# Slice weights of a graph network: a third buffer of normalised rows, and another order of the turned tiles on TensorE

## The reference

```python
x_mid = (x @ W_x + b_x).reshape(B, N, H, D).transpose(0, 2, 1, 3)      # H = 8 heads of 64
temp = jnp.clip(temperature, 0.1, 5.0)
slice_weights = jax.nn.softmax((x_mid @ W_slice + b_slice) / temp, axis=-1)
slice_norm = slice_weights.sum(axis=2)
slice_token = jnp.einsum('bhnc,bhng->bhgc', fx_mid, slice_weights)
slice_token = slice_token / (slice_norm[..., None] + 1e-05)
# attention among the 64 slice tokens of each head gives out_slice
out_x = jnp.einsum('bhgc,bhng->bhnc', out_slice, slice_weights)
```

## Time and profile before

| | |
|---|---|
| median of 3 runs | 7850.16 us (7850.01 to 7862.31) |
| the profiled execution, time | 7849.75 us |
| its span in the trace | 7848.0 us |
| busy in the span | PE 69%, DVE 66%, POOL 44%, ACT 24% |
| `slice_weights` | 3558 to 3888 us of the span |

### The profile page before, as it was taken

The page is one execution under the profiler, slowest core; times in us unless marked ns, Lnnn a source line. Parts: engine busy times, 40 slices in busy tenths (PEclk is TensorE's granted clock), DMA queues, the critical chain, the costliest instruction groups (busy, mean ns, idle before and its releaser), DMA issues. The chain is left out here.

```text
span 7848.0 us, 86538 instructions
## 1 busy us (share of the span) xinstructions
PE 5431.4 (69%) x24766; PEld 3747.1 (48%) x24766; DVE 5164.8 (66%) x11681; ACT 1874.3 (24%) x4564; POOL 3485.0 (44%) x3441
## 2 busy tenths in 40 slices
PE   5877774555555555517799788888899999951991
PEld 2446663333333443314464333433777778750661
DVE  6457767888888877774467566676666767660332
ACT  0333332222223333212224200000222222210220
POOL 0000004777777777710000355555666777716006
PEclk8998886777777777759999899999999999965995
DMA  4100003444455555530013322222333333332223
GB/s 143 45 27 1 1 1 95 124 124 124 124 126 128 128 131 129 136 60 3 6 68 132 117 75 73 72 75 77 87 94 94 98 97 97 97 70 83 64 63 107
DMA packets 310188, 665.87 MB, mean 85 GB/s; under 512 B 77974, under 2 KB 173964, under 8 KB 302717
## 3 DMA queue, kind: packets, MB, share of 16 engines
q0 software_dynamic: 180352, 455.22, 23.0%
q1 hardware_dynamic: 129383, 205.31, 7.6%
HBM read 546.52 MB, written 113.55 MB: 84 GB/s over the span
## 5 line engine op out<-in xcount | busy, mean ns | idle before, releaser
L2055 POOL DMA_INDIRECT ag_rows<-table,row_src x1612 | 1595.8, 990 | 1896.5 <-POOLq L2847 1023.5
L1142 POOL DMA_INDIRECT at_rows<-table,row_dst x1612 | 1645.5, 1021 | 491.3 <-issue 450.8
L1308 PE MATMUL at_p_a<-at_rows,at_hot 128*125 128x264 f32 x3224 | 1132.0, 509 | 1014.6 <-issue 972.1
L1308 PEld LDWEIGHTS at_p_a<-at_rows,at_hot 128*125 128x125 f32 x3224 | 706.0, 245 | 1201.7 <-issue 1062.5
L2422 PE MATMUL mo_p_e<-ag_rows,ag_hot 128*125 128x256 f32 x2192 | 650.9, 422 | 293.9 <-DVE acc L2263 257.2
L1271 DVE TENSOR_TENSOR acc<-acc,at_p_a 125x264 f32 x1612 | 687.1, 426 | 245.0 <-PE at_p_a L1308 101.8
L2263 DVE TENSOR_TENSOR acc<-acc,mo_p_e 125x256 f32 x1096 | 459.0, 419 | 442.9 <-PE mo_p_e L2422 243.1
L2422 PEld LDWEIGHTS mo_p_e<-ag_rows,ag_hot 128*125 128x125 f32 x2192 | 391.5, 199 | 503.1 <-DVE acc L2263 394.8
L2165 DVE TENSOR_TENSOR mo_prod<-mo_far,mo_twice 125x256 f32<-125x256 f32 x1600 | 580.4, 419 | 51.6 <-issue 45.1
L1094 POOL PARTITION_ALL_REDUCE sb_top<-sb_top x1 | 0.4, 398 | 1220.8 <-DVE sb_top L1065 1220.8
L1258 DVE TENSOR_TENSOR at_rows<-at_rows 128x1024 f32<-128x1024 f32 x496 | 496.2, 1021 | 21.9 <-ACT at_rows L1190 21.6
(11 more groups left out here) (491 smaller groups left out, 9751.8 us busy)
## 6 DMA issues: line engine op xcount, KB each, us to landing
at_wide<-node_t SPq DMA_DIRECT2D x124, 406.2 KB
table<-rt_row SPq DMA_DIRECT2D x50, 1000.0 KB
at_rows<-table,row_dst POOLq DMA_INDIRECT x1612
ag_rows<-table,row_src POOLq DMA_INDIRECT x1612
moe_in<-ones SPq DMA_DIRECT2D x1, 13440.0 KB
ex_space<-moe_in SPq DMA_DIRECT2D x105, 128.0 KB, 2.2
moe_out<-ex_space SPq DMA_DIRECT2D x105, 128.0 KB, 1.7
table<-row SPq DMA_DIRECT2D x50, 128.9 KB
```

What stands on the lines that cost most here:

```text
L1142: pool.indirect_dma_start(out=rows[n % 3][:, g, :], out_offset=None, in_=m.table0, in_offset=bass.IndirectOffsetOnAxis(ap=row_i[:, n * G + ...
L1308: pe.matmul(p_a[k % BANKS][0:P, 0:TW], hot[n % 2][:, g, :], rows[n % 3][:, g, :], start=True, stop=True).then_inc(s_agg, 1)
L2055: pool.indirect_dma_start(out=rows[:, i % RING, j, :], out_offset=None, in_=m.table1, in_offset=bass.IndirectOffsetOnAxis(ap=row_i[:, 2 * ...
```

## The change

There are three buffers `sl_xn` instead of two. ACT normalises tile n+2 behind exp(n), and copies its turned tile behind swt(n). PE runs logits(n+1), W(n), turn(n+2), S(n) in step n, so that the turned rows are made two tiles ahead and stand between the turned weights and the sums. The two loops of PE, ACT and the loop of DVE are written out.

```diff
-        xn = [sb(f"sl_xn{u}", [P, C + 1], F32) for u in range(2)]
+        xn = [sb(f"sl_xn{u}", [P, C + 1], F32) for u in range(3)]
...
-                def front(n, u):
-                    if later(n):
-                        act.wait_ge(s_sum, n - 1)
-                    act.activation(xn[u][:, 0:C], m.x[:, n, :], ACT.Identity, scale=m.rstd[:, bass.ds(n, 1)],
-                                   bias=m.nmr[:, bass.ds(n, 1)]).then_inc(s_xn, 1)
+                def norm(n):
+                    if n >= 3:
+                        act.wait_ge(s_sum, n - 2)
+                    act.activation(xn[n % 3][:, 0:C], m.x[:, n, :], ACT.Identity, scale=m.rstd[:, n:n + 1],
+                                   bias=m.nmr[:, n:n + 1]).then_inc(s_xn, 1)
+
+                def copy_xt(n):
                     act.wait_ge(s_tr, n + 1)
-                    act.copy(xt[u][:, :, :].rearrange("p c n -> p (c n)"), p_t[:, 0:2 * P]).then_inc(s_xt, 1)
-
-                front(0, 0)
-
-                def step(n, u, last):
-                    if not last:
-                        front(n + 1, 1 - u)
+                    if n >= 2:
+                        act.wait_ge(s_log, n - 1)
+                    act.copy(xt[n % 2][:, :, :].rearrange("p c n -> p (c n)"), p_t[:, 0:2 * P]).then_inc(s_xt, 1)
+
+                norm(0)
+                copy_xt(0)
+                norm(1)
+                copy_xt(1)
+                for n in range(NT):
                     act.wait_ge(s_sub, n + 1)
-                    act.activation(w[u][:, :], w[u][:, :], ACT.Exp).then_inc(s_exp, 1)
+                    act.activation(w[n % 2][:, :], w[n % 2][:, :], ACT.Exp).then_inc(s_exp, 1)
+                    if n + 2 < NT:
+                        norm(n + 2)
                     act.wait_ge(s_wt, n + 1)
-                    act.copy(swt[:, bass.ds(n, 1), :, :].rearrange("p a o n -> p (a o n)"), p_w[:, 0:4 * P]).then_inc(s_swt, 1)
-
-                in_units_last(act, step)
+                    act.copy(swt[:, n, :, :].rearrange("p o n -> p (o n)"), p_w[:, 0:4 * P]).then_inc(s_swt, 1)
+                    if n + 2 < NT:
+                        copy_xt(n + 2)
...
-                in_units(dve, step, NT)
+                for n in range(NT):
+                    step(n, n % 2)
...
-                def front(n, u):
+                def turn(n):
                     pe.wait_ge(s_xn, n + 1)
-                    if not first(n):
+                    if n >= 1:
                         pe.wait_ge(s_xt, n)
...
+                def logits(n):
                     pe.wait_ge(s_xt, n + 1)
-                    if later(n):
+                    if n >= 2:
                         pe.wait_ge(s_sub, n - 1)
...
+                turn(0)
+                turn(1)
+                logits(0)
+                for n in range(NT):
+                    if n + 1 < NT:
+                        logits(n + 1)
                     pe.wait_ge(s_sw, n + 1)
-                    if not first(n):
+                    if n >= 1:
                         pe.wait_ge(s_swt, n)
                     for o in range(4):
-                        mm = pe.transpose(p_w[:, P * o:P * o + P], w[u][:, 128 * o:128 * o + 128], m.ident[0:P, 0:P])
+                        mm = pe.transpose(p_w[:, P * o:P * o + P], w[n % 2][:, 128 * o:128 * o + 128], m.ident[0:P, 0:P])
                     mm.then_inc(s_wt, 1)
+                    if n + 2 < NT:
+                        turn(n + 2)
                     for o in range(4):
-                        mm = pe.matmul(p_s[o][:, 0:C + 1], w[u][:, 128 * o:128 * o + 128], xn[u][:, :],
+                        mm = pe.matmul(p_s[o][:, 0:C + 1], w[n % 2][:, 128 * o:128 * o + 128], xn[n % 3][:, :],
                                        start=False, stop=False, skip_group_check=True)
                     mm.then_inc(s_sum, 1)
-
-                in_units_last(pe, step)
```

More of the change, by code:

```diff
@@ L1488, in _ @@
                 act.wait_ge(s_zero, 1)
-                def front(n, u):
-                    if later(n):
-                        act.wait_ge(s_sum, n - 1)
-                    act.activation(xn[u][:, 0:C], m.x[:, n, :], ACT.Identity, scale=m.rstd[:, bass.ds(n, 1)],
-                                   bias=m.nmr[:, bass.ds(n, 1)]).then_inc(s_xn, 1)
-                    act.wait_ge(s_tr, n + 1)
-                    act.copy(xt[u][:, :, :].rearrange("p c n -> p (c n)"), p_t[:, 0:2 * P]).then_inc(s_xt, 1)
-                front(0, 0)
-                def step(n, u, last):
-                    if not last:
-                        front(n + 1, 1 - u)
+                def norm(n):
[4 more added lines that the diff above has]
+                def copy_xt(n):
+                    act.wait_ge(s_tr, n + 1)
+                    if n >= 2:
[6 more added lines that the diff above has]
+                for n in range(NT):
                     act.wait_ge(s_sub, n + 1)
-                    act.activation(w[u][:, :], w[u][:, :], ACT.Exp).then_inc(s_exp, 1)
+                    act.activation(w[n % 2][:, :], w[n % 2][:, :], ACT.Exp).then_inc(s_exp, 1)
+                    if n + 2 < NT:
+                        norm(n + 2)
                     act.wait_ge(s_wt, n + 1)
-                    act.copy(swt[:, bass.ds(n, 1), :, :].rearrange("p a o n -> p (a o n)"), p_w[:, 0:4 * P]).then_inc(s_swt, 1)
-                in_units_last(act, step)
+                    act.copy(swt[:, n, :, :].rearrange("p o n -> p (o n)"), p_w[:, 0:4 * P]).then_inc(s_swt, 1)
+                    if n + 2 < NT:
+                        copy_xt(n + 2)
             @block.vector
             def _(dve):
-                for u in range(2):
+                for u in range(3):
                     dve.memset(xn[u][:, C:C + 1], 1.0)
@@ L1542, in _ @@
                     pe.matmul(p_s[o][:, 0:C + 1], zero[:, 0:128], zero[:, :], start=True, stop=False, skip_group_check=True)
-                def front(n, u):
+                def turn(n):
                     pe.wait_ge(s_xn, n + 1)
-                    if not first(n):
+                    if n >= 1:
                         pe.wait_ge(s_xt, n)
                     for c in range(2):
-                        mm = pe.transpose(p_t[:, P * c:P * c + P], xn[u][:, 128 * c:128 * c + 128], m.ident[0:P, 0:P])
+                        mm = pe.transpose(p_t[:, P * c:P * c + P], xn[n % 3][:, 128 * c:128 * c + 128], m.ident[0:P, 0:P])
@@ L1550, in front @@
                     mm.then_inc(s_tr, 1)
+                def logits(n):
                     pe.wait_ge(s_xt, n + 1)
-                    if later(n):
+                    if n >= 2:
                         pe.wait_ge(s_sub, n - 1)
                     for c in range(2):
-                        pe.matmul(p_l[u][0:P, :], xt[u][:, c, :], w_log[:, c, :], start=c == 0, stop=False)
-                    pe.matmul(p_l[u][0:P, :], m.ones3[:, 0:P], b_log[:, :], start=False, stop=True).then_inc(s_log, 1)
@@ L1558, in _ @@
[L1558 to L1562, removed]
+                        pe.matmul(p_l[n % 2][0:P, :], xt[n % 2][:, c, :], w_log[:, c, :], start=c == 0, stop=False)
+                    pe.matmul(p_l[n % 2][0:P, :], m.ones3[:, 0:P], b_log[:, :], start=False, stop=True).then_inc(s_log, 1)
+                turn(0)
[4 more added lines that the diff above has]
+                        logits(n + 1)
```

## The result

| | before | changed |
|---|---|---|
| median of 4 runs each | 7850.09 us (7849.85 to 7862.31) | 7752.24 us (7746.15 to 7758.76) |
| ratio | | 0.9871, 95% interval 0.9856 to 0.9885 |
| span of the profiled execution | 7848.0 us | 7744.4 us |

The kernel became faster by 1.29%, or 101 us of 7850. I had forecast 89 (7760.8). The median stands inside my range, 3 us from its lower end, but the ratio, applied to 7850.1, gives 7748.8: the gain is just past the end of what I allowed. The profile says that the stage did what was forecast, and that the surplus does not come from it.

The account below looks back on a forecast made before the run. The prediction took slice_weights as a ring of waits at 6.47 us a tile; PE's terms 0.22 + 1.74 + 1.81 + 0.36 + 0.48 = 4.61 would save 89.0 us: 7849.75 - 89.0 = 7760.8 us, range 7749 to 7785.

Parts of the forecast that it names:

- PE paces the stage at 4.61 us a tile: In slice_weights, PE's own work sets the rate after the change: 4.61 us a tile, bounds 4.37 to 4.81; 76%.
- the five terms: PE's work per tile in slice_weights: turn 0.22, sums 1.74, logits 1.81, bias to next transpose 0.36, turned weights 0.48 us.
- both joints: On PE in slice_weights, the steps turn to sums and sums to logits, taken as free; otherwise 4.81 us a tile.
- Everything else fits, slack 0.57: In slice_weights, tile n's weights are ready at 4.04 us against 4.61, the smallest slack; ACT is no bound.
- the signs: What the profile after should show in slice_weights, including DVE idle before top about 0.5 us a tile.
- Start and end: First and last tiles of slice_weights: W(0), the first turned weights, at 3570.52; W(49), the last, at 3795.9.
- Saved in the stage 89.0: In slice_weights, the last turned weights come at 3795.9 instead of 3884.87, saving 89.0 us.
- Loops written out cost nothing and are worth nothing: In slice_weights, loop rounds cost 0.14 us more, at most 3 us, no separate term; supplying the longer code costs nothing.
- the old ring: In slice_weights before, two sl_xn buffers make norm(n+1) wait for sums(n-1); 6.47 us a tile with no engine full.
- So all later work moves as one piece: Behind slice_weights, the whole 89.0 us saving arrives at the kernel's end, giving 7760.8 us.
- Rivals 2 to 4: 2: DVE and ACT pace slice_weights, 16%; 3: little or no gain, 3%; 4: written-out code supplied too late, slower, 2%.
- Rival 5: More gain than forecast, by a better clock in the stage behind slice_weights, total under 7749 us; 3%.

Follow-up runs that it names:

- e11: The kernel before, unchanged, profiled once more on a slower chip: stage 328.9 us, relational_mix 2774.3 us.

## Why the prediction was right or wrong

- *PE paces the stage at 4.61 us a tile*: right, 4.60; each of the five terms to 0.01, both joints free. Removing the bias confirms from the other side that PE sets the pace.
- *Everything else fits, slack 0.57*: right, 0.55 from the end of DVE's product to the weight load. With this slack DVE has to stand idle 0.7 us before top, which is what the changed kernel shows (0.72); my "about 0.5" in the signs didn't follow from my own sum.
- *Start and end*: W(0) at 3570.4 (3570.5), W(49) at 3795.3 (3795.9).
- *Saved in the stage 89.0*: 89.5.
- *Loops written out cost nothing and are worth nothing*: right in the changed kernel, for they are worth nothing with PE at the pace; but my price for them in the old ring (3 us) was too low, 9 us. Both rounds of the loop carried the loop's cost, 0.14 and 0.27 us against 6.27 without it, and I read the shorter as free of it. It did no harm, since the sum was made from starts and not from this price.
- *"So all later work moves as one piece"*: this step failed. It does, for some 900 us. In `relational_mix` the clock is granted at 0.5 in some stretches and not in others, and not in the same ones from one execution to the next. In the first pair of profiles this was worth 14 us to the changed kernel, with 30 us less at the lower clock; over the runs of the slower chips it is worth nothing that I can tell from 0, and on the faster ones a remainder of 7 to 11 us is left whose cause is open. I put 3% on a gain beyond 7749 and made 7749 the end of the range, out of 4.37 us a tile, a bound for the stage; the scatter of the runs themselves had no term in it. I had seen three runs of the kernel before, two of which agreed to 0.15 us. The earlier trace rows and the clock in other windows had shown me that it falls in places, and I asked only whether it falls in `slice_attention`.
- Rivals 2 to 4 are refused: the stage's pace is PE's, the gain is there, and the one gap of 0.37 us that the written-out code shows in DVE hides in its slack. Rival 5, more than forecast, is the one that came nearest, but the clock did it in `relational_mix`; in `slice_attention`, right behind the stage, the time at the lower clock is 41 us in both.

That the low clock costs the time is argued from 13 profiles, from PE's busy and idle time in them, and from the length of the same transposes at both levels; no edit held the clock up or down, so it isn't shown by experiment. What decides where it falls stays open.

No kernel was faster than the changed one but the one without the bias, which leaves work out.

## What to carry to other kernels

A ring with no full engine is opened by finding the buffer that closes it, and then the queue order that uses the new one: here the buffer alone gave 44 us of 89 (against the kernel with its loops written out), the order alone none, and both together gave the 89 in a loop too. Price the state after it from start to start in rows where the same instructions run back to back; that was good to 0.01 us a term. And give the range a term for what the rest of the kernel does by itself: look for stages where the granted clock changes from one level to the other, for there a shorter stage ahead, or nothing at all, moves the total by more than 10 us.

## What was unexpected in the hardware

- One and the same program, profiled twice on one chip, took 8337.3 and 8300.5 us, with the clock at 0.809 and 0.813; the 72 us more at the lower level cost 31 us in one stage.
- A bf16 matmul of 512 columns between fp32 matmuls costs PE 0.44 us (4.60 against 4.16 us a tile), twice its columns: 0.09 us before it and about 0.15 behind it.
- Two chips took 14% longer in `attend` and 10% longer in `relational_mix`, and the same time elsewhere. In `attend` nearly all of it is PE standing idle (1344 us in e11 against 1049 in the first profile), with more time at the lower clock (1592 against 1213); in `relational_mix` some of it is longer matmuls.
- With its code written out, DVE stood idle one to three times in the stage's rounds for about 0.4 us with no releaser (ten profiles); in a loop of two tiles it never did (three).
